# Graph attention of a two-layer model: eight probability tiles instead of four, copies six units back, and a reciprocal taken over 512 columns

## The chip, the core and the metric

The kernel runs on one core of a Trainium2 chip. The metric is the device time of one execution in microseconds (us). One execution was recorded by the hardware profiler, and its trace is what is read below. PE is the matrix engine (PEld its weight loads), DVE the vector engine, ACT the scalar engine, POOL the general engine; SP issues most of the DMAs.

## The reference

The model has two layers over `x`, four batches of 512 tokens by 512 columns. Only the first of its four blocks is touched, a two-layer graph attention with 8 heads of 64 columns:

```python
def gat_layer(x, adj, W, a_self, a_neigh, b):
    feat = jnp.einsum('nf,hfo->hno', x, W)
    attn_self = jnp.einsum('hno,ho->hn', feat, a_self)
    attn_neigh = jnp.einsum('hno,ho->hn', feat, a_neigh)
    e = attn_self[:, :, None] + attn_neigh[:, None, :]
    e = jax.nn.leaky_relu(e, LRELU_ALPHA)
    e = e + MASK_VAL * (1.0 - adj)[None, :, :]
    alpha = jax.nn.softmax(e, axis=-1)
    out = jnp.einsum('hnm,hmo->hno', alpha, feat) + b[:, None, :]
    out = jnp.transpose(out, (1, 0, 2)).reshape(out.shape[1], -1)
    return jax.nn.elu(out)
...
x = x + _L0_xattn_ref(ctx_512, _layernorm(x, axis=-1), ...)   # gat_layer twice, per batch
x = x + _L0_ffn_ref(...)
x = x + _L1_xattn_ref(...)
x = x + _L1_ffn_ref(...)
```

The mask `adj` is the normalised `x` itself, so every element of the 512 x 512 scores is used. Everything is float32 in this block.

## The kernel before

`graph_attention` is the first stage of five; a barrier stands between it and the mixture of experts that follows. Its work is cut into 256 **units**: 8 phases (4 batches times 2 layers; the order is layer 0 of batches 0 and 1, layer 1 of the same, then the same for batches 2 and 3), in each phase 8 heads, in each head 4 tiles of 128 tokens. Eight units, that is two heads, make a **pair**; there are 32 pairs, 4 in a phase.

All engines run the same hand-written loop over n, the unit, and each engine's queue is in program order. One unit goes through: `add_neighbours` on POOL (L283, a ring of LAG = 4 tiles `near`); `relu` on ACT (L459, two PSUM banks, issued two units ahead and behind the exponential of unit n in ACT's queue); `masked` on DVE (L544, makes `eneg` and its minimum); the exponential on ACT (L474, into `prob`, a ring of 4, with the row sums into `rsum`); four transposes on PE (L365, two PSUM banks `pt_bank`, each waiting until DVE has copied the unit two before); `copy_probT` on DVE (L553), which DVE issues COPY_LAG = 3 units after that unit's `masked`.

Once per pair, `finish` does the rest, spread over steps counted from the end of the pair's last unit. DVE takes the reciprocal of the pair's 128 x 8 row sums (L561, step 1). PE turns it into a 128 x 512 tile by eight 128 x 64 matmuls against the identity, with a broadcast operand (L383, step 2; float32 matmuls leave two records each, so x16), and ACT copies that to `rall` (L486). PE multiplies probabilities and features into `o_bank` (L397, steps 4 and 5, sixteen records). DVE multiplies `o_bank` by `rall` (L566, step 8), makes `zmax` (L570, step 9), ACT takes an exponential in place (L491), DVE joins them (L577, step 11). In layer 1 PE turns the result back (L405, step 13), DVE adds the old tokens (L582, step 15), and POOL stores them by DMA (L270) and loads the next ones (L265).

Beside this, `prepare(k, n)` makes the next phase's inputs during the current phase: on PE a product with the attention vectors (L338 for a layer 1, n from 10), four small transposes (L345, n = 17), the features (L355, one product a unit from n = 15 to 30 when the next phase is layer 1, four in all when it is layer 0); on DVE L534 (n = 16) and L537 (n = 18); on ACT the copies of the features (L442, n = 19, 23, 27, 31), each of which waits for the PE product of the unit before. In phases 0, 3 and 4 DVE, ACT and POOL also normalise the mask of a later batch (L511 to L527, L446, L261), and in phase 0 DVE weighs the second layer's weights (L503, L505).

Of the kernel before, what the change touches and what calls it, by code (L numbers as in the profile page):

```python
# [11 lines left out]
P = 128  # L12
RING = 2
# [5 lines left out]
ACT = mybir.ActivationFunctionType  # L19
# [56 lines left out]
def graph_attention(nc, x, ctx_dram, W0, a_self0, a_neigh0, b0, W1, a_self1, a_neigh1, b1, t_dram, x1):  # L76
# [13 lines left out]
    COPY_LAG = 3  # L90
    PREP_FIRST, PREP_FEAT = 10, 15
# [7 lines left out]
    def out_pair(pr):  # L99
        half, rest = divmod(pr, 2 * SLOTS * PAIRS)  # L100
        return half * SLOTS * PAIRS + rest - SLOTS * PAIRS

# [3 lines left out]
    with ExitStack() as stack:  # L106
# [102 lines left out]
        with nc.Block() as block:  # L209
# [39 lines left out]
            def _(pool):  # L249
# [37 lines left out]
                for n in range(ALL_UNITS + 3 * PAIR):  # L287
# [9 lines left out]
                    pr, step = divmod(n - 3 * PAIR, PAIR)  # L297
                    if 0 <= pr < ALL_PAIRS and phase(pr // PAIRS)[1] == 1:
                        j = out_pair(pr)
                        if step == 5:  # L300
                            store_new(j)
                        if step == 7 and j + RING < OUT_PAIRS:
                            pool.wait_ge(xo_stored[j % RING], 16 * (j // RING + 1))
                            load_old(j + RING)
# [5 lines left out]
            def _(pe):  # L310
                pe.wait_ge(consts, 1)

                def prepare(k, n):
# [27 lines left out]
                    if n == PREP_FEAT + 2:  # L341
# [18 lines left out]
                def transposes(n):  # L360
                    if n >= PT_BANKS:
                        pe.wait_ge(pt_ready, n - PT_BANKS + 1)
                    pe.wait_ge(p_ready, n + 1)
                    for c in range(NT):
                        last = nc.tensor.transpose(pt_bank[n % PT_BANKS][:, c, :], prob[:, n % LAG, c * P:(c + 1) * P], ident[:, :])  # L365
                    last.then_inc(pt_ps, 1)

                def finish(pr, step):

                    k, pair = divmod(pr, PAIRS)  # L370
                    if step == 2:

                        pe.wait_ge(rinv_ready, pr + 1)
                        if pr:
                            pe.wait_ge(rall_ready, pr)
                            before = pr - 1
                            if phase(before // PAIRS)[1] == 1 and out_pair(before) >= 1:
                                pe.wait_ge(xo_ready, out_pair(before))
                            elif phase(before // PAIRS)[1] == 0 and before >= 2 * SLOTS * PAIRS:
                                pe.wait_ge(xo_ready, before // (2 * SLOTS * PAIRS) * SLOTS * PAIRS)  # L380
# [6 lines left out]
                    if step == 4:  # L387
# [5 lines left out]
                    if step in (4, 5):  # L393
                        for c in range(step % 4 * 2, step % 4 * 2 + 2):
# [6 lines left out]
                    if step == PAIR + 5 and phase(k)[1] == 1:  # L401
# [6 lines left out]
                for n in range(PREP_FIRST, UNITS):  # L408
                    prepare(0, n)
                for n in range(ALL_UNITS):  # L410
                    transposes(n)
                    if n >= PAIR:
                        finish(n // PAIR - 1, n % PAIR)
                    if n >= 2 * PAIR:
                        finish(n // PAIR - 2, n % PAIR + PAIR)
                    if n // UNITS + 1 < PHASES:
                        prepare(n // UNITS + 1, n % UNITS)
                for step in range(PAIR):
                    finish(ALL_PAIRS - 1, step)
                    finish(ALL_PAIRS - 2, step + PAIR)  # L420
                for step in range(PAIR, 2 * PAIR):
                    finish(ALL_PAIRS - 1, step)

            @block.scalar
            def _(act):
# [8 lines left out]
                def prepare(k, n):  # L434
                    batch, layer, slot = phase(k)
                    if n == PREP_FIRST + 2 and layer == 0:
# [25 lines left out]
                for n in range(PREP_FIRST, PREP_FEAT + NT + 1):  # L462
                    prepare(0, n)
                root(0)
                for n in range(PREP_FEAT + NT + 1, UNITS):
                    prepare(0, n)
                for n in range(H_BANKS):
                    relu(n)
                for n in range(ALL_UNITS + 2 * PAIR):
                    if n < ALL_UNITS:  # L470
                        act.wait_ge(e_ready, n + 1)
                        if n >= LAG:
                            act.wait_ge(pt_ps, n - LAG + 1)
                        nc.scalar.activation(prob[:, n % LAG, :], eneg[:, n % LAG, :], ACT.Exp, scale=-1.0, bias=emin[:, n % LAG:n % LAG + 1],  # L474
# [6 lines left out]
                    if PAIR <= n < ALL_UNITS + PAIR and n % PAIR == 4:  # L481
# [5 lines left out]
                    if n >= 2 * PAIR and n % PAIR == 2:  # L487
# [4 lines left out]
                    if n // UNITS + 1 < PHASES:  # L492
                        prepare(n // UNITS + 1, n % UNITS)

            @block.vector
            def _(dve):
# [32 lines left out]
                def prepare(k, n):  # L529
                    if n == PREP_FEAT + 1:  # L530
# [4 lines left out]
                    if n == PREP_FEAT + 3:  # L535
# [19 lines left out]
                def finish(pr, step):  # L555
# [11 lines left out]
                    if step == PAIR + 1:  # L567
# [3 lines left out]
                    if step == PAIR + 3:  # L571
# [6 lines left out]
                    if step == PAIR + 7 and layer:  # L578
# [9 lines left out]
                prepare(0, PREP_FEAT + 1)  # L588
                mask_statistics(0)
                prepare(0, PREP_FEAT + 3)  # L590
# [7 lines left out]
                for n in range(ALL_UNITS + 2 * PAIR):  # L598
# [4 lines left out]
                    if n >= 2 * PAIR:  # L603
                        finish(n // PAIR - 2, n % PAIR + PAIR)
                    if n >= PAIR and n < ALL_UNITS + PAIR:
                        finish(n // PAIR - 1, n % PAIR)
                    if n // UNITS + 1 < PHASES:
                        prepare(n // UNITS + 1, n % UNITS)
# [1429 lines left out]
```

## Time and profile before

| what | us |
|---|---|
| median of three runs | 2299.05 (2295.28 to 2305.4) |
| the profiled execution, its own time | 2292.93 |
| its span, first to last instruction | 2291.1 |
| graph attention, first `masked` to the end of the last L582 (29.2 to 617.9) | 588.7 |
| DVE busy in that stage | about 431 |
| PE busy in that stage | about 460 |

How to read the profile: a row of the timeline gives start, duration, engine, line and operation, and in brackets how long the engine had been idle before and what ended the idleness.
### The profile page before, as it was taken

How to read it: one execution, taken by the hardware profiler on the slowest of the kernel's cores; microseconds unless marked ns; L12 is line 12 of the kernel's file. 1: busy time of each engine (PE TensorE's matmuls, PEld its weight loads, DVE VectorE, ACT ScalarE, POOL GpSimd, SP SyncE). 2: the span in 40 equal slices, each digit the busy share in tenths (PEclk: the TensorE clock that was granted, in tenths of full speed). 3: DMA queues.
4: the chain of work that ended last, by engine and by line, in shares of the span. 5: the costliest groups of instructions: out<-in, count | busy, mean ns of one | idle time of the engine just before them, and what ended most of it. 6: DMA issues, size and time to landing. Idle time of an engine off the chain costs nothing. (4 is left out here: it accounts for less than half of the span.)

```text
span 2291.1 us, 33610 instructions
## 1 busy us (share of the span) xinstructions
PE 1850.8 (81%) x8271; PEld 911.1 (40%) x8272; DVE 1461.1 (64%) x3126; ACT 1050.8 (46%) x1893; POOL 881.7 (38%) x949
## 2 busy tenths in 40 slices
PE   5598776888547999999992388888889439999994
PEld 2343433444344555555551122222222414444442
DVE  5777766777585565555654477777775675555552
ACT  5577766777432232232323256666667422222221
POOL 5465665656402545555542211111111013444441
PEclk8799877999777999999995589999999759999997
DMA  5111211110263789888656921111111626888984
GB/s 139 51 38 38 71 59 56 38 38 29 67 211 95 178 182 232 217 190 211 113 93 170 173 54 52 52 51 51 50 50 33 230 80 178 230 226 230 230 214 107
DMA packets 202160, 275.34 MB, mean 120 GB/s; under 512 B 83500, under 2 KB 121868, under 8 KB 200972
## 3 DMA queue, kind: packets, MB, share of 16 engines
q1 hardware_dynamic: 156395, 170.72, 24.2%
q0 software_dynamic: 38544, 97.02, 21.0%
q10 hardware_dynamic: 7121, 6.44, 1.4%
q8 instruction: 43, 0.70, 0.1%
q14 instruction: 57, 0.47, 0.1%
HBM read 204.44 MB, written 73.37 MB: 121 GB/s over the span
## 5 line engine op out<-in xcount | busy, mean ns | idle before, releaser
L1891 DVE TENSOR_REDUCE a_negmax<-a_m 128x1 f32<-128x512 f32 x512 | 328.1, 686 | 108.8 <-PE a_m L1748 107.2
L283 POOL TENSOR_TENSOR g_near<-g_mask,g_tb 128x512 f32<-128x512 f32 x256 | 322.8, 1277 | 156.2 <-DVE g_emin L544 154.2
L1840 ACT ACTIVATE a_prob<-a_s 128x1024 f32<-128x1024 f32 x256 | 260.6, 1021 | 142.4 <-PE a_s L1759 134.9
L365 PE MATMUL g_pt<-g_ident,g_p 128*128 128x128 f32 x1024 | 189.6, 319 | 125.9 <-DVE g_pT L553 115.7
L1283 PE MATMUL f_gu_bank<-f_wgu,f_xT 128*128 x768 | 267.9, 492 | 6.5 <-issue 3.8
L1748 PE MATMUL a_m<-a_kT,a_qT 112*128 (+1 forms) x512 | 198.7, 399 | 72.0 <-DVE a_negmax L1891 38.7
L474 ACT ACTIVATE g_p<-g_e,g_emin 128x512 f32<-128x512 f32 x256 | 183.3, 716 | 125.3 <-DVE g_emin L544 123.4
L1249 POOL DMA_INDIRECT tokens<-f_y,f_ids x96 | 151.2, 1575 | 222.5 <-DMA tokens<-f_y,f_ids 186.1
L1283 PE MATMUL s_gu_bank<-s_wgu,s_xT 128*128 128x512 f32 x512 | 232.3, 597 | 2.3 <-ACT s_xT L1335 1.6
L365 PEld LDWEIGHTS g_pt<-g_ident,g_p 128*128 128x128 f32 x1024 | 130.7, 160 | 252.9 <-DVE g_pT L553 199.7
L544 DVE CUSTOM_DVE_ANT_0 g_e<-g_near,g_h 128x512 f32<-128x512 f32 x256 | 173.2, 677 | 58.6 <-issue 28.0
L1283 PEld LDWEIGHTS f_gu_bank<-f_wgu,f_xT 128*128 128x128 f32 x768 | 143.5, 191 | 137.3 <-issue 58.3
L553 DVE COPY g_pT<-g_pt 128x512 f32<-128x512 f32 x256 | 175.4, 685 | 14.7 <-PE g_pt L365 14.1
L1302 PE MATMUL f_y_bank<-f_wd,f_actT 96*128 x384 | 183.3, 600 | 1.5 <-DVE f_actT L1368 0.9
L1249 POOL DMA_INDIRECT tokens<-s_y,s_ids x64 | 101.6, 1588 | 198.7 <-ACT s_y L1341 198.4
L459 ACT ACTIVATE g_h<-g_tb,g_s 128x512 f32<-128x512 f32 x256 | 172.8, 675 | 0.0
L1759 PE MATMUL a_s<-a_qT,a_kT 115*128 115x512 bf16 x512 | 153.8, 383 | 1.5 <-DMA a_qT<-a_mrows 1.4
L1368 DVE COPY f_actT<-f_at_bank 96x256 f32<-96x256 f32 x96 | 40.4, 421 | 175.0 <-PE f_at_bank L1292 175.0
L1283 PEld LDWEIGHTS s_gu_bank<-s_wgu,s_xT 128*128 128x128 f32 x512 | 97.8, 192 | 125.3 <-issue 125.0
L1748 PEld LDWEIGHTS a_m<-a_kT,a_qT 112*128 112x128 bf16 x512 | 49.6, 97 | 243.4 <-DVE a_negmax L1891 162.1
L1225 POOL DMA_INDIRECT f_row<-f_x_rows,f_ids x96 | 101.9, 1062 | 106.7 <-issue 104.2
L1771 PE MATMUL a_o<-a_prob,a_val 128*32 128x512 f32 x1024 | 136.4, 605 | 0.4 <-ACT a_prob L1840 0.4
(295 smaller groups left out, 2811.5 us busy)
## 6 DMA issues: line engine op xcount, KB each, us to landing
s_wgu<-in_L_ffn_w_gate_up SPq DMA_DIRECT2D x32, 1024.0 KB, 7.5
f_wgu<-in_L_ffn_gate_up_proj SPq DMA_DIRECT2D x32, 768.0 KB, 6.0
s_wd<-in_L_ffn_w_down SPq DMA_DIRECT2D x32, 512.0 KB, 4.1
a_qT<-q_parts SPq DMA_DIRECT2D x217, 64.0 KB, 2.2
g_tb<-neighbours SPq DMA_DIRECT2D x8, 1536.0 KB, 7.6
f_wd<-in_L_ffn_down_proj SPq DMA_DIRECT2D x32, 384.0 KB, 5.4
q_parts<-p_part SPq DMA_DIRECT2D x48, 128.0 KB, 2.3
g_tb<-neighbours SPq DMA_DIRECT2D x8, 512.0 KB, 4.3
```

Of the source, the lines that this page charges most:

```text
L283: pool.tensor_tensor(near[:, n % LAG, :], mask[slot][:, local % NT, :], t_all[k % SLOTS][:, local // NT, :], ALU.add).then_inc(near_ready, 1)
L365: last = nc.tensor.transpose(pt_bank[n % PT_BANKS][:, c, :], prob[:, n % LAG, c * P:(c + 1) * P], ident[:, :])
L459: nc.scalar.activation(h_bank[n % H_BANKS][:, :], t_all[k % SLOTS][:, h, :], ACT.Relu, scale=4.0, bias=s_high[k % SLOTS][:, t, h:h + 1]).t ...
L474: nc.scalar.activation(prob[:, n % LAG, :], eneg[:, n % LAG, :], ACT.Exp, scale=-1.0, bias=emin[:, n % LAG:n % LAG + 1], accum_out=rsum[:, ...
L544: V.tensor_tensor_reduce(out=eneg[:, n % LAG, :], in0=near[:, n % LAG, :], in1=h_bank[n % H_BANKS][:, :], scale=-1.0, scalar=3.0e38, op0=A ...
L553: V.tensor_copy(probT[:, n // PAIR % RING, hh, :, t * P:(t + 1) * P], pt_bank[n % PT_BANKS][:, :, :]).then_inc(pt_ready, 1)
L1249: pool.indirect_dma_start(out=tokens, out_offset=bass.IndirectOffsetOnAxis(ap=ids[:, j:j + 1], axis=0), in_=y[j % YR][:, :], in_offset=Non ...
L1283: last = nc.tensor.matmul(gu_bank[k % TR][:, 0:F], xT[k % TR][:, c, :], wgu[:, bass.ds(place, 1), c, :].rearrange("p a f -> p (a f)"), sta ...
L1302: last = nc.tensor.matmul(y_bank[k % TR][:, :], actT[k % TR][:, c, :], wd[:, bass.ds(place, 1), c, :].rearrange("p a f -> p (a f)"), start ...
L1748: nc.tensor.matmul(m_bank[n % RING][:, :], qT[k][0:PAIR_ROWS, head, st * P:(st + 1) * P], group_keys(G, PAIR_ROWS, slice(0, N)), start=Tru ...
L1840: nc.scalar.activation(prob[n % QR][:, :, :], s_bank[n % RING][:, :, :], ACT.Exp).then_inc(p_ready, 1)
L1891: V.tensor_reduce(negmax[k % RING][:, st, head:head + 1], m_bank[n % RING][:, :], X_AXIS, ALU.max, negate=True).then_inc(m_read, 1)
```

## The change

The ring `prob` grows from 4 tiles to 8 and DVE copies a unit's transposed probabilities six units back instead of three. `rinv` becomes 128 x (4, 2, 64): DVE's reciprocal reads each of the eight sums 64 times and writes 512 columns, and PE turns it by four 128 x 128 transposes in place of the eight 128 x 64 products. The steps of `finish` move: on PE the turning of the reciprocal from step 2 to 0, the products from 4 and 5 to 2, 3 and 4 (halves, then quarters), the layer-1 transposes from 13 to 11; on ACT the copy to `rall` from 4 to 5 and the exponential of `o_bank` from 2 to 3 of the pair after; on DVE L566 from 8 to 10, L570 from 9 to 11, L577 from 11 to 13, L582 from 15 to 17. In `prepare`, PE starts at n = 8 instead of 10 and makes the small transposes at 15 instead of 17; ACT copies features at 24, 28, 32 and 36 (the last two in the next phase) instead of 19 to 31; DVE's two scalings stand at 17 and 21. POOL stores at the last unit of the pair and loads two units later, each later by two. The diff without the loops that only follow:

```diff
-    COPY_LAG = 3
-    PREP_FIRST, PREP_FEAT = 10, 15
+    PROBS, COPY_LAG = 8, 6
+    STEPS = 3 * PAIR
+    SUMS = {2: range(0, 2), 3: range(2, 3), 4: range(3, 4)}
+    PREP_FIRST, PREP_FEAT, PREP_END = 8, 15, 40
...
-        prob = sb("g_p", [P, LAG, N])
+        prob = sb("g_p", [P, PROBS, N])
...
-        rinv = sb("g_ri", [P, RING, PAIR])
+        rinv = sb("g_ri", [P, RING, NT, 2, F_OUT])
...
-                    if step == 2:
+                    if step == 0:
...
-                        for u in range(PAIR):
-                            t, hh = divmod(u, 2)
-                            last = nc.tensor.matmul(r_bank[hh * F_OUT:(hh + 1) * F_OUT, t, :],
-                                                    bass.AP(rinv, pr % RING * PAIR + hh * NT + t, [[RING * PAIR, P], [0, F_OUT]]), ident[:, :],
-                                                    start=True, stop=True)
+                        for t in range(NT):
+                            last = nc.tensor.transpose(r_bank[:, t, :], rinv[:, pr % RING, t, :, :].rearrange("p h o -> p (h o)"), ident[:, :])
...
-                    if step in (4, 5):
-                        for c in range(step % 4 * 2, step % 4 * 2 + 2):
+                    if step in SUMS:
+                        for c in SUMS[step]:
...
-                    if step == PAIR + 5 and phase(k)[1] == 1:
+                    if step == PAIR + 3 and phase(k)[1] == 1:
...
-                    t, rest = divmod(n - PREP_FEAT - NT, NT)
+                    t, rest = divmod(n - PREP_FEAT - 9, NT)
...
-                        if n >= LAG:
-                            act.wait_ge(pt_ps, n - LAG + 1)
+                        if n >= PROBS:
+                            act.wait_ge(pt_ps, n - PROBS + 1)
...
-                    if PAIR <= n < ALL_UNITS + PAIR and n % PAIR == 4:
+                    if PAIR <= n < ALL_UNITS + PAIR and n % PAIR == 5:
...
-                        V.reciprocal(rinv[:, pr % RING, :], rsum[:, pr % RING, :]).then_inc(rinv_ready, 1)
-                    if step == PAIR:
+                        V.reciprocal(rinv[:, pr % RING, :, :, :], bass.AP(rsum, pr % RING * PAIR, [[RING * PAIR, P], [1, NT], [NT, 2], [0, F_OUT]])).then_inc(rinv_ready, 1)
+                    if step == PAIR + 2:
...
-                    if step == PAIR + 1:
+                    if step == PAIR + 3:
...
-                    if step == PAIR + 3:
+                    if step == PAIR + 5:
...
-                    if step == PAIR + 7 and layer:
+                    if step == 2 * PAIR + 1 and layer:
```

## Rows read from the trace of the kernel before

**Rows 1.** Windows: length, busy us of PE, PEld, DVE, ACT, POOL, granted clock: the stage.
```profile
29.20:620.00 590.80, 459.79 (x2342) 238.76 (x2342) 431.23 (x984) 403.55 (x871) 351.46 (x299) 0.86 0.15 48
```

**Rows 2.** Waits of DVE, 30 to 620 us: total us, times, longest.
```profile
DVE g_xo L582 <- PE g_r L405: 46.0, 16, 4.4
DVE g_e L544 <- issue: 28.0, 12, 2.9
DVE g_e L544 <- ACT g_h L459: 26.1, 37, 1.7
DVE g_o L566 <- PE g_o L397: 15.8, 14, 1.3
DVE g_pT L553 <- PE g_pt L365: 14.1, 15, 2.1
DVE g_s L537 <- PE g_f L345: 9.5, 7, 1.7
DVE g_xT L577 <- ACT g_o L491: 7.2, 13, 1.2
DVE g_res L577 <- issue: 5.2, 12, 1.2
```

**Rows 3.** Groups by line, shapes apart: the reciprocals of DVE, three widths.
```profile
L1381 DVE RECIPROCAL f_den<-f_den 128x192 f32<-128x192 f32 x96 | 129.9, 1353 | 3.3
L1381 DVE RECIPROCAL s_den<-s_den 128x256 f32<-128x256 f32 x64 | 112.2, 1753 | 2.2
...
L561 DVE RECIPROCAL g_ri<-g_rs 128x8 f32<-128x8 f32 x32 | 6.0, 189 | 0.0
```

**Rows 4.** Windows by pair, from one reciprocal of L561 to the next.
```profile
162.68:179.73 17.05, 16.38 (x80) 7.43 (x79) 12.36 (x30) 12.72 (x29) 10.17 (x8) 1.00 0.00 0
...
211.39:230.30 18.91, 17.54 (x91) 8.39 (x90) 12.68 (x31) 12.03 (x27) 10.14 (x9) 1.00 0.30 111
...
406.72:420.31 13.59, 9.65 (x66) 5.19 (x64) 11.94 (x30) 11.84 (x27) 10.10 (x9) 1.00 0.00 0
...
557.63:574.04 16.41, 12.49 (x70) 7.47 (x68) 12.54 (x31) 11.98 (x27) 11.50 (x11) 0.80 0.12 34
```

**Rows 5.** Timeline of DVE inside one pair with features being prepared.
```profile
169.28 0.68 DVE L544 CUSTOM_DVE_ANT_0 g_e<-g_near,g_h 128x512 f32<-128x512 f32 x1
...
169.88 0.69 DVE L553 COPY g_pT<-g_pt 128x512 f32<-128x512 f32 x1
...
177.05 0.70 DVE L566 TENSOR_TENSOR g_o<-g_o,g_rall 128x512 f32<-128x512 f32 x1 [1.09 <-PE g_o L397]
177.66 0.68 DVE L544 CUSTOM_DVE_ANT_0 g_e<-g_near,g_h 128x512 f32<-128x512 f32 x1
```

**Rows 6.** Timeline of ACT: a feature copy waiting for PE.
```profile
162.28 0.60 ACT L442 ACTIVATE g_feat<-g_f 128x512 f32<-128x512 f32 x1 [3.37 <-PE g_f L355]
```

**Rows 7.** Timeline of PE, at full clock and then at half.
```profile
174.99 1.94 PE L397 MATMUL g_o<-g_pT,g_feat 128*64 128x512 f32 x8
...
184.49 1.09 PE L383 MATMUL g_r<-g_ident,g_ri 128*64 128x128 f32 x16
...
575.45 2.32 PE L365 MATMUL g_pt<-g_ident,g_p 128*128 128x128 f32 x8 [1.28 <-DVE g_pT L553]
577.70 1.98 PE L383 MATMUL g_r<-g_ident,g_ri 128*64 128x128 f32 x16
```

**Rows 8.** Windows of 1.7 us, PE alone: busy, granted clock.
```profile
571.60:573.30 1.70, 0.66 (x4) 1.00 0.00 0
...
575.00:576.70 1.70, 1.16 (x5) 0.50 0.51 154
...
580.10:581.80 1.70, 1.70 (x9) 0.62 0.00 0
```

**Rows 9.** Timeline of DVE: its last two additions of the stage.
```profile
612.37 0.69 DVE L582 TENSOR_TENSOR g_xo<-g_r,g_xo 128x512 f32<-128x512 f32 x1 [4.42 <-PE g_r L405]
...
617.20 0.69 DVE L582 TENSOR_TENSOR g_xo<-g_r,g_xo 128x512 f32<-128x512 f32 x1 [1.27 <-PE g_r L405]
```

More of the change, by code:

```diff
@@ L101, in out_pair, with pairs_at, preparing_at @@
         return half * SLOTS * PAIRS + rest - SLOTS * PAIRS
+    def pairs_at(n):
+        return [pr for pr in range(n // PAIR - 3, n // PAIR) if 0 <= pr < ALL_PAIRS]
+    def preparing_at(n):
+        return [k for k in (n // UNITS, n // UNITS + 1) if 0 < k < PHASES]
     def mask_phase(m):
@@ L286, in _ @@
                     mask_tile(0, t)
-                for n in range(ALL_UNITS + 3 * PAIR):
+                for n in range(ALL_UNITS + 5 * PAIR):
                     if n < ALL_UNITS:
@@ L296, in _ @@
                             load_old(j)
[L297 to L304, printed above, removed]
+                    for back in (3, 4):
+                        pr = n // PAIR - back
+                        if 0 <= pr < ALL_PAIRS and phase(pr // PAIRS)[1] == 1:
+                            j = out_pair(pr)
+                            if back == 3 and n % PAIR == PAIR - 1:
+                                store_new(j)
+                            if back == 4 and n % PAIR == 1 and j + RING < OUT_PAIRS:
+                                pool.wait_ge(xo_stored[j % RING], 16 * (j // RING + 1))
+                                load_old(j + RING)
                 for r in range(RING):
@@ L364, in transposes @@
                     for c in range(NT):
-                        last = nc.tensor.transpose(pt_bank[n % PT_BANKS][:, c, :], prob[:, n % LAG, c * P:(c + 1) * P], ident[:, :])
+                        last = nc.tensor.transpose(pt_bank[n % PT_BANKS][:, c, :], prob[:, n % PROBS, c * P:(c + 1) * P], ident[:, :])
                     last.then_inc(pt_ps, 1)
@@ L375, in finish @@
                             pe.wait_ge(rall_ready, pr)
[L376 to L380, printed above, removed]
-                        for u in range(PAIR):
-                            t, hh = divmod(u, 2)
-                            last = nc.tensor.matmul(r_bank[hh * F_OUT:(hh + 1) * F_OUT, t, :],
-                                                    bass.AP(rinv, pr % RING * PAIR + hh * NT + t, [[RING * PAIR, P], [0, F_OUT]]), ident[:, :],
-                                                    start=True, stop=True)
+                            turned = sum(1 for p in range(pr - 1) if phase(p // PAIRS)[1] == 1)
+                            if turned:
+                                pe.wait_ge(xo_ready, turned)
+                        for t in range(NT):
+                            last = nc.tensor.transpose(r_bank[:, t, :], rinv[:, pr % RING, t, :, :].rearrange("p h o -> p (h o)"), ident[:, :])
                         last.then_inc(r_ps, 1)
-                    if step == 4:
+                    if step == 2:
                         pe.wait_ge(pt_ready, PAIR * (pr + 1))
@@ L406, in finish @@
                         last.then_inc(ot_ps, 1)
-                for n in range(PREP_FIRST, UNITS):
+                for n in range(PREP_FIRST, PREP_END):
                     prepare(0, n)
[L410 to L422, printed above, removed]
+                for n in range(ALL_UNITS + STEPS):
+                    if n < ALL_UNITS:
+                        transposes(n)
+                    for pr in pairs_at(n):
+                        finish(pr, n - PAIR * (pr + 1))
+                    for k in preparing_at(n):
+                        prepare(k, n - UNITS * (k - 1))
             @block.scalar
@@ L529, in prepare @@
                 def prepare(k, n):
-                    if n == PREP_FEAT + 1:
+                    if n == PREP_FEAT + 2:
                         dve.wait_ge(stT_ps, k + 1)
@@ L597, in _ @@
                 dve.wait_ge(bias_done, 1)
-                for n in range(ALL_UNITS + 2 * PAIR):
+                for n in range(ALL_UNITS + STEPS):
                     if n < ALL_UNITS:
@@ L602, in _ @@
                         copy_probT(n - COPY_LAG)
[L603 to L608, printed above, removed]
+                    for pr in pairs_at(n):
+                        finish(pr, n - PAIR * (pr + 1))
+                    for k in preparing_at(n):
+                        prepare(k, n - UNITS * (k - 1))
                     w = n - (UNITS - 2 * FC)
```

22 lines of the change are left out of this document (11 added, 11 removed).

## The prediction

> **What bounds the kernel now.** The first view is the windows by stage: the change touches only the graph attention, 591 us of the 2291 us span, and in it no engine is full, PE 460 us busy, DVE 431, ACT 404, POOL 351 [rows 1]. So the stage is bound by hand-overs between queues, and the next view is who waits for whom. DVE is the engine to follow: all others wait for it in nearly every unit, and each pair's work ends in it. Its waits [rows 2] add up to about 155 us with the small ones: 46.0 for the layer-1 transposes (L582), 28.0 in front of `masked` with no engine named, 26.1 in front of `masked` for ACT's relu, 15.8 for the products (L566), 14.1 for transposes of probabilities, 9.5 for the small transposes, 12.4 in front of L577 (7.2 + 5.2).
>
> The windows by pair give the same as a budget [rows 4]. A pair takes 13.6 us where nothing is prepared in layer 0, 16.4 in layer 1, 17.05 and 18.9 where features are prepared; DVE is busy for 11.9 to 12.7 us of each. The rest, 1.7 to 6.2 us, is what a better order can give back. PE is busy for 16.4 to 17.5 us in the pairs with features, 9.7 in the light ones.
>
> **The reciprocal, the largest term.** L561 takes 189 ns for 8 columns. Two wider reciprocals of this trace take 1353 ns for 192 and 1753 ns for 256 columns [rows 3]: 400 ns for 64 columns, 6.25 ns a column. For 512 that is 1753 + 256 x 6.25 = 3353 ns; started from the 8-column row it is 189 + 504 x 6.25 = 3339. The input with repeated elements reads no more than the wider ones did, and I see no row that would make it cheaper or dearer; I take 3.35 us. DVE gains 3.16 us a pair, 32 x 3.16 = **+101 us**. As a bound I let it go 5% either way (96 to 106).
>
> This trace shows 6.25 ns a column. The Trainium skill, page "VectorE: DVE Perf Modes", section "First, the fixed hardware budget", says that the reciprocal is an iterative division with a repeat count of 8, and gives DVE's clock as 0.96 GHz; read as eight cycles a column, that would be an estimate of 512 x 8 / 0.96 = 4.27 us, and the sum would be some 29 us worse. The trace does not agree with that reading.
>
> Nothing hides this work. It stands in DVE's queue, at unit 1 of each pair; behind it wait `masked` of the next unit (and so ACT's exponential and relu, POOL's ring) and the next copy (and so PE's transposes). DVE's budget for a pair becomes 11.9 + 3.2 = 15.1 us in layer 0 and 12.5 + 3.2 = 15.7 us in layer 1, against 13.6 to 18.9 now.
>
> **What PE saves** is real but off the path. The sixteen records of L383 took 1.09 us at full clock [rows 7]; four transposes start about 0.55 us apart, group after group. That is 0.5 us a pair, 17 us in all, on an engine that mostly waits for DVE. I count it at 0; where features are prepared it is part of what lets the pair shrink.
>
> **What the moved steps give back.** I walk the queues with the steps of the trace: `masked` 0.60 and copy 0.61 from start to start, 0.61 for L566 [rows 5].
> - L582 waited 2.9 us each time, since PE issued its transposes at step 13, after a transpose group that DVE had only just released, and DVE wanted them at 15. Now they are at 11 and 17, so they end about when the copy that DVE does before L582 can start. 46.0 less the drain's waits (4.42 + 1.27 in [rows 9], and an estimated 3.7 for the one before them, between these two and the mean of 2.9) is 36.6: all gone, **-37**.
> - L566 waited for the products at steps 4 and 5, issued two to four units earlier on DVE's clock. Now the last quarter is at 4 and L566 at 10, while the copies are three units later: one unit of margin is gained. **-16**.
> - L537 comes six units after its transposes instead of one, of which three go to the later copies: **-9.5**. L577 comes two units after ACT's exponential as before, but that exponential is no longer behind a late zmax or a feature copy: **-12**.
> - The relu: ACT idled up to 3.37 us for a feature product [rows 6], with the relu behind it. The copies of the features go from one unit behind the product to six, three of them used up by PE's later place. I take 18 of 26.1: **-18**. The rest I leave, as ACT's own pace: its exponential, its read of the sums and its relu together take more than DVE's 1.21 us a unit.
> - The 28 us with no name are the rows where POOL turns the mask tile by tile between DVE and its own additions in phases 0, 3 and 4. Order and count are the same: **0**.
> - The ring of eight removes ACT's wait for the transposes four back. No wait of that kind stood ahead of DVE's, so it is worth 0 alone; it is what allows copies six back.
> Sum of what is given back: 37 + 16 + 9.5 + 12 + 18 = **-92 us**.
>
> **What is added as waits.** While DVE divides, copy n-5 is late. From the end of copy n-6 to that of n-5 it is 3.34 + 0.60 + 0.61 = 4.5 us, in which PE may do at most two groups of transposes (two banks) and what stands with them.
> - In the pairs with features PE has a backlog: it is busy for 16.4 us now, tails of its groups included [rows 4], so about 15.9 against DVE's 15.1. But three PE units (products 1.9, 1.0, 1.0, from the 1.94 of a half in [rows 7]) fall together where DVE runs its fastest units. By the walk DVE waits 0.6 us there, just in front of the reciprocal; eight such pairs, +5.
> - In the light pairs PE has nothing to do for 4 us and then one group of 0.66 us per 1.2 to 1.9 us until the products. Today a stretch of that kind drops the granted clock: PE was busy for 0.66 us in 1.7 [rows 8] for about 5 us, the clock fell from 1.00 to 0.50, and only some 5 us of full work brought it back; meanwhile eight transposes took 2.32 us and the sixteen records of L383 1.98 instead of 1.09 [rows 7]. The thin stretch is now some 6.5 us, in nearly every light pair, layer 0 too, where it was 3.4 us and the clock stayed at 1.00 [rows 4]. At half clock a half of the products takes 3.5 us instead of 1.9, and DVE's copy of the third unit waits. The walk gives 0.5 to 2.7 us; I take 1.3 for ten pairs, +13, and 2 for the four pairs where PE also has the L338 products in the same units, +8.
>
> The Trainium skill, page "TensorE: Matmul & The Clock Gate", section "HAM oscillation — how this bites in real kernels", describes a kernel whose matrix engine dropped to half clock in every round because of a regular idle gap. It speaks against this change: where it holds, the +21 of the last item stands, and where it does not, that term is 0.
>
> Together +26, in place of the 14.1 us of waits for transposes that stand at the same spots now: **+12 us** (bounds: -14 if PE never is late, +54 if each of 27 pairs pays 2.5 us, the walk's upper end, less the 14).
>
> **The drain.** The stage ends with a serial chain [rows 9]. Three more copies are behind the last `masked` (1.8 us), and the last reciprocal, already counted, is in the chain. **+2**; bounds 0 and +6. The start issues three copies less before the first pair and is counted there.
>
> **Sum**: 101 - 92 + 12 + 2 = **+23 us**, 1.0% of the kernel. Against the profiled execution's own time it is 2292.9 + 23 = 2316; the median of the three runs is 6.1 us above that execution, and what is compared is medians, so 2299 + 23 = **2322 us**.
>
> **Rivals.**
> 1. *Not slower: the waits go and the clock holds.* If PE never falls to half clock, the added waits are 5 instead of 26, and the 14.1 us go with them: 101 - 92 - 9 + 2 = +2, 2301 us. For it: pairs of layer 0 kept 1.00 with PE busy for 9.65 of 13.59 us [rows 4]. Against: the thin stretch doubles. It decides at whether PE's clock is at 1.00 when the first products of a light pair start. Chance 0.22.
> 2. *Faster: DVE becomes full.* All waits but the drain's and the mask's go, 155 - 9 - 28 = 118 us: 101 - 118 + 2 = -15, and the relu's pace, hidden in "busy" at about 0.1 us in some units, could add as much again: 2270 to 2284 us. It needs every hand-over right in 31 pairs and a full clock, or a reciprocal that is cheaper than its neighbours. Chance 0.12.
> 3. *PE at half clock bounds the pairs.* With 2.5 us of waiting in all 27 pairs: 101 - 92 + 54 + 2 = +65, 2364 us. Against: with features prepared PE is full and keeps 1.00 [rows 4]. Chance 0.06.
> 4. *The division is eight cycles a column*, as the page named above can be read. As a mechanism of this kernel, from rows: each reciprocal would be longer by a fraction of the 3.35 us, and if by a quarter, 32 x 0.84 = 27 us on DVE's path, 2349 us. [Rows 3] speaks against it. Chance 0.04.
>
> **How the numbers follow.** The forecast case has 0.56 and its own range of 2306 to 2345. The measurement tells about 0.5%, 11.5 us, from no change. Of the forecast's 0.56, 0.06 lies under +11.5; with rival 1 that is 0.28 for the same; rival 2 is 0.12 faster; 0.50 + 0.06 + 0.04 = 0.60 slower. The range is **2286 to 2354**: it takes in rivals 1 and 4 and leaves out most of rivals 2 and 3.
>
> **What would show it.** Right: L561 at 3.35 us and DVE busy in the stage at some 530 us; no waits of L582 for L405 but in the drain; ACT's 50 us of waiting for features mostly gone; light pairs of layer 0 longer than 13.6 us, at 15 to 17; pairs with features shorter, near 16 to 17; PE's clock below 1.00 in light pairs, with DVE's copies waiting for L365. Wrong: an L561 clearly off 3.35 us; waits for transposes beyond 40 us; or pairs at DVE's bare 15.1 us.

## The result and the profile after

| | before | after |
|---|---|---|
| median us | 2299.05 (9 runs, 2295.28 to 2305.4) | 2308.52 (9 runs, 2303.83 to 2313.36) |
| the profiled execution, its own time | 2292.93 | 2313.36 |
| its span | 2291.1 | 2311.6 |
| graph attention, first `masked` to the end of the last addition | 588.7 | 601.7 |

The ratio is 1.0043, with a 95% interval of 1.0033 to 1.0052: the changed kernel is slower by 9.5 us (8 to 12). The forecast was 2322, +23 us: the sign was right, the size more than double what was measured.

The two profiled executions differ by more than the medians, 20.4 us: 13.0 of them in the stage, 1.6 before it (the first `masked` starts at 30.8 us instead of 29.2), and the rest in the four later stages. What comes behind the graph attention took between 1672.5 and 1684.0 us in the thirteen profiles of this case, in no order that follows the changes, so a difference of some us between two profiled times says nothing by itself.

Line numbers have moved: `masked` is L542, the copy L551, the reciprocal L559, its turning on PE L389, the transposes L374, the products L401, the addition of the old tokens L580. First the groups by line of the changed kernel, in the first 720 us: count, busy us, mean ns of one, idle us before it and who ended it.

```profile
L551 DVE COPY g_pT<-g_pt 128x512 f32<-128x512 f32 x256 | 175.5, 686 | 35.2 <-PE g_pt L374 35.1
...
L559 DVE RECIPROCAL g_ri<-g_rs 128x512 f32<-128x512 f32 x32 | 107.0, 3343 | 0.0
...
L389 PE MATMUL g_r<-g_ident,g_ri 128*128 128x128 f32 x128 | 27.9, 360 | 0.0
```

The wide reciprocal takes 3343 ns, between the two estimates drawn from [rows 3] (3339 and 3353); it adds 107.0 - 6.0 = 101.0 us to DVE. Next the waits of DVE in the changed kernel's stage, which answer to [rows 2].

```profile
DVE g_pT L551 <- PE g_pt L374: 35.1, 32, 2.7
DVE g_e L542 <- issue: 26.4, 12, 2.9
DVE g_e L542 <- ACT g_h L457: 7.1, 19, 1.0
...
DVE g_xo L580 <- PE g_r L409: 5.1, 2, 4.3
DVE g_e L542 <- POOL g_near L291: 3.5, 4, 2.0
DVE g_o L564 <- PE g_o L401: 1.3, 1, 1.3
```

Against [rows 2], the addition waits 5.1 us instead of 46.0 (the two that are left are the drain's), the products 1.3 instead of 15.8, the relu 7.1 instead of 26.1, the scaling behind the small transposes (L537 before, L535 now) nothing instead of 9.5. ACT's waits for the feature products went from 49.9 us to 14.6. Waits for the transposes of probabilities grew from 14.1 to 35.1. Last, windows of single pairs in the changed kernel: length, busy us of PE, PEld, DVE, ACT and POOL, granted clock.

```profile
150.51:170.21 19.70, 16.93 (x68) 8.40 (x66) 15.73 (x32) 11.64 (x25) 10.15 (x8) 0.83 0.31 109
...
410.03:426.17 16.14, 12.50 (x56) 6.67 (x54) 14.99 (x30) 13.47 (x31) 10.77 (x9) 0.79 0.00 0
...
170.21:186.12 15.91, 15.56 (x70) 7.35 (x68) 14.98 (x29) 12.40 (x29) 10.02 (x8) 1.00 0.00 1
```

DVE is now busy for 15.0 us of a 15.9 or 16.1 us pair. In the light pairs it has become the fullest engine; in the pair with features PE, busy for 15.56 of 15.91 us, is fuller still. The light pair of layer 0 that took 13.59 us in [rows 4] takes 16.14; the pair with features that took 17.05 takes 15.91. The second pair of a phase with features, 19.70 us, is the worst in this profile; PE's clock is 0.83 of full there.

**The ledger.** In the stage, DVE busy plus DVE waits is the length. Before: 431.2 + 157.4 = 588.6. After: 523.0 + 79.6 = 602.6, within 1 us of the stage's 601.7. (Both waits are summed over all rows of the view, the small ones too.) So busy grew by 92 and the waits shrank by 78.

### The profile page after: what moved, and what is told of

Read it like the earlier page. It is cut to its first block and busy times, and to the rows that moved or that the text cites. A ratio compares the mean times of both kernels' runs of the same rounds, so it can differ in the third digit from the quotient of the medians.

```text
span 2311.6 us, 32838 instructions
## 1 busy us (share of the span) xinstructions
PE 1848.7 (80%) x7887; PEld 900.5 (39%) x7888; DVE 1553.9 (67%) x3126; ACT 1049.2 (45%) x1893; POOL 882.2 (38%) x949
## 5 line engine op out<-in xcount | busy, mean ns | idle before, releaser
L374 PE MATMUL g_pt<-g_ident,g_p 128*128 128x128 f32 x1024 | 195.3, 323 | 145.0 <-DVE g_pT L551 140.1
L374 PEld LDWEIGHTS g_pt<-g_ident,g_p 128*128 128x128 f32 x1024 | 135.3, 163 | 288.8 <-DVE g_pT L551 225.1
L551 DVE COPY g_pT<-g_pt 128x512 f32<-128x512 f32 x256 | 175.5, 686 | 35.2 <-PE g_pt L374 35.1
L542 DVE CUSTOM_DVE_ANT_0 g_e<-g_near,g_h 128x512 f32<-128x512 f32 x256 | 172.7, 675 | 37.9 <-issue 26.4
L1755 PE MATMUL a_s<-a_qT,a_kT 115*128 115x512 bf16 x512 | 154.0, 383 | 3.6 <-DMA a_qT<-a_mrows 3.5
L401 PE MATMUL g_o<-g_pT,g_feat 128*64 128x512 f32 x512 | 144.5, 668 | 1.4 <-DVE g_res L575 1.4
```

Source lines behind the costliest of these rows:

```text
L542: V.tensor_tensor_reduce(out=eneg[:, n % LAG, :], in0=near[:, n % LAG, :], in1=h_bank[n % H_BANKS][:, :], scale=-1.0, scalar=3.0e38, op0=A ...
L551: V.tensor_copy(probT[:, n // PAIR % RING, hh, :, t * P:(t + 1) * P], pt_bank[n % PT_BANKS][:, :, :]).then_inc(pt_ready, 1)
```

## The experiments

All times are medians, beside runs of the kernel before on the same chip (2297 to 2299 us).

### The two halves of the change, each alone

```diff
 narrow_recip: the changed kernel with
...
-                        for t in range(NT):
-                            last = nc.tensor.transpose(r_bank[:, t, :], rinv[...], ident[:, :])
+                        for u in range(PAIR):
+                            last = nc.tensor.matmul(r_bank[...], bass.AP(rinv, ..., [[RING * PAIR, P], [0, F_OUT]]), ident[:, :], ...)
...
-                        V.reciprocal(rinv[:, pr % RING, :, :, :], bass.AP(rsum, ..., [[RING * PAIR, P], [1, NT], [NT, 2], [0, F_OUT]]))
+                        V.reciprocal(rinv[:, pr % RING, :], rsum[:, pr % RING, :])
...
 wide_old_order: the kernel before, with the reverse of these edits and nothing else
```

> The changed kernel with the reciprocal and its turning undone: L559 takes 8 columns again (0.19 us for 3.34) and PE turns it by eight broadcast products; ring of eight, copies six back and all steps stay. Theory A (the order gives back some 95 us of DVE's waits, and the wide reciprocal sits in DVE's full queue and costs nearly its whole 101 us): 2308.5 - 101 and about 20 us of waits come back where PE's own work, 16 to 17 us a pair with features, now ends last: some 2225 us, 3.6% below the changed kernel and 3.2% below the one before. Theory B (the order gives little by itself, and the reciprocal is hidden behind PE): within 1% of the changed kernel, 2285 to 2310.

> The kernel before with only the wide reciprocal and the four transposes, in the old order. Theory A: DVE gains 101 us and PE catches up during the division, which takes away the 14 us of waits for transposes and some of the 46 us in front of L582: 2299 + 75 to 95, about 2385. If the two parts add up, this one's distance from the kernel before equals that of the changed kernel from the one with the narrow reciprocal. Theory B (hidden behind PE and the waits): under 2330.

Measured: the new order with the narrow reciprocal takes **2239.33 us** (ratio to before 0.9746, 0.9732 to 0.9761), the old order with the wide one **2400.70** (1.0439, 1.042 to 1.0458). Theory B falls: the order is worth 59 us, and the wide reciprocal undoes it. Theory A has the direction of both, but misses both sizes, with 2225 expected for the first and about 2385 for the second: the two parts do not add as it had them. On the old order the wide reciprocal costs 102 us, all of DVE's added 101; on the new order it costs 2308.5 - 2239.3 = 69 us. In the old order PE does not use the division to catch up: DVE's waits stay at 163 us over all rows (157 before), the addition's 48.9 us among them.

The waits of DVE with the narrow reciprocal say why the new order is different (here L554 is the copy, L567 the multiplication of the products, L460 the relu).

```profile
DVE g_pT L554 <- PE g_pt L374: 42.6, 39, 2.1
...
DVE g_o L567 <- PE g_o L404: 8.5, 20, 1.3
DVE g_e L545 <- ACT g_h L460: 7.9, 17, 1.8
```

The order took away most of the same waits as in the changed kernel, but a part came back as waiting for PE's transposes, 42.6 us. All rows together are 99.3 us of waits, against 79.6 with the wide reciprocal; DVE is busy for 427.3 us, against 523.0. One pair with features shows the bound: length, then PE busy, the same number.

```profile
149.96:166.03 16.07, 16.07 (x82) 8.01 (x80) 12.15 (x29) 12.89 (x29) 10.14 (x8) 1.00 0.00 0
```

That pair takes 16.07 us with the narrow reciprocal and 15.91 with the wide one. So in a pair where PE is full the wide form as a whole costs nothing. That does not say that the division alone is hidden: the wide form also gives PE four transposes in place of sixteen records, and the last experiment below, with the short DVE work and PE's four transposes, does this pair in 15.29 us. In the light pairs the wide form costs most of the division's 3.2 us: the two of layer 0 that take 15.57 and 16.14 us in the changed kernel (15.19 and 15.19 in its second profile) take 12.80 and 14.00 here, and the first two without any preparation in the last phase 12.91 and 13.86 instead of 16.75 and 16.91 (15.83 and 16.39).

### Twice the division

```diff
...
+                        V.reciprocal(rinv[...], bass.AP(rsum, ...)).then_inc(rfirst_done, 1)
+                        dve.wait_ge(rfirst_done, pr + 1)
                         V.reciprocal(rinv[...], bass.AP(rsum, ...)).then_inc(rinv_ready, 1)
```

> The changed kernel with the wide reciprocal done twice (second one waits for the first), nothing left out; DVE gains another 32 x 3.3 = 106 us. From 8 columns to 512 the first 101 us of DVE cost 69 us of time. Theory E (below a certain load DVE's added work replaces waiting for PE, above it DVE is full): the second dose costs nearly all of its 106 us, at least 95, 2405 to 2420, and the waits for transposes do not grow by more than 10 us. Theory F (a fixed share of any added division is hidden behind PE): it costs about 70 us again, 2380.

Measured 2415.87 us, 107 above the changed kernel (2308.5), for 108 us of added DVE work (busy in the stage 630.6 against 523.0); waits for transposes 35.9 us, as before it. That is what Theory E had: beyond the load of the changed kernel each further us of DVE costs a us. The step from the narrow form to the wide one cost 69 us for 101 us of division, the next 107 cost 107. Theory E puts the missing 32 us down to DVE's load; the saving on PE, which came with the first step and not with the second, is a rival that this run does not separate (see the narrow reciprocal with a wide copy, below).

### Is it the clock? PE kept busy

```diff
-                    for c in range(NT):
+                    light = n % UNITS < 15 or n % UNITS == UNITS - 1 or (n // UNITS) % 4 in (0, 3)
+                    for c in list(range(NT)) * ({5: 3, 6: 3, 7: 3, 0: 2}.get(n % PAIR, 1) if light else 1):
                         last = nc.tensor.transpose(pt_bank[n % PT_BANKS][:, c, :], ...)
```

> The changed kernel with PE kept busy in its thin stretches: where no feature product follows, the transposes of the pair's units 5, 6 and 7 are done three times over and those of unit 0 twice, into the same bank; 768 transposes less those in feature units are added, and nothing is left out. Theory A1 (DVE's 35 us of waits for transposes come from PE at half clock): PE's clock in the pairs of layer 0 rises from 0.8 to near 1.0 and these waits fall to about 15 us, the whole to about 2290. Theory A2 (they come from PE's amount of work where products stand together): the clock rises, the waits stay at 35 us or grow, 2305 to 2325.

Measured **2291.45 us** (12 runs; ratio to before 0.9974, 0.996 to 0.9988): 17 us less than the changed kernel, by adding 672 transposes that compute nothing new. Waits for transposes fell from 35.1 to 19.5 us. The timeline of PE in the changed kernel shows what it cures, in the pair of 19.70 us:

```profile
153.36 0.66 PE L374 MATMUL g_pt<-g_ident,g_p 128*128 128x128 f32 x4
155.64 0.66 PE L374 MATMUL g_pt<-g_ident,g_p 128*128 128x128 f32 x4 [1.62 <-DVE g_pT L551]
157.44 1.10 PE L374 MATMUL g_pt<-g_ident,g_p 128*128 128x128 f32 x4 [1.15 <-DVE g_pT L551]
...
158.99 2.08 PE L364 MATMUL g_f<-g_w,g_xT 128*128 128x512 f32 x2
```

DVE divides from 150.5 to 153.9 us, and the copies behind the division come late. PE works on until 154.0 and then has one group of 0.66 us after 1.62 us of idleness and the next after 1.15; at 157.4 us its clock is at half (a group takes 1.10 us instead of 0.66, a feature product 2.08 instead of 1.02), and the dear work of the pair starts at that clock.

The fall does not come every time. In the second profile of the changed kernel the same two gaps stand at the same place of the same pair, and the clock holds:

```profile
156.56 0.66 PE L374 MATMUL g_pt<-g_ident,g_p 128*128 128x128 f32 x4 [1.62 <-DVE g_pT L551]
158.36 0.66 PE L374 MATMUL g_pt<-g_ident,g_p 128*128 128x128 f32 x4 [1.15 <-DVE g_pT L551]
...
159.29 1.12 PE L364 MATMUL g_f<-g_w,g_xT 128*128 128x512 f32 x2
```

So a single pair proves nothing, as this one takes 19.70 us in one profile and 16.57 in the other, and the first two pairs of the four phases in which features for layer 1 are prepared have to be taken together (us from one reciprocal to the next):

| | the changed kernel | its second profile | PE kept busy |
|---|---|---|---|
| first pair of the phase | 17.88, 19.26, 17.88, 19.26 | 19.25, 18.27, 18.69, 18.85 | 16.92, 16.91, 16.91, 16.92 |
| second pair | 19.70, 17.17, 19.70, 17.17 | 16.57, 18.64, 18.14, 18.74 | 16.56, 17.16, 16.57, 17.16 |

These eight pairs take 148.0 and 147.2 us without the edit and 135.1 with it, at full clock in all eight.

```profile
149.80:166.36 16.56, 15.54 (x84) 8.15 (x82) 15.46 (x31) 11.50 (x25) 10.07 (x8) 1.00 0.36 128
```

Theory A1 stands. The rule of the Trainium skill that the prediction weighed ("TensorE: Matmul & The Clock Gate", section "HAM oscillation — how this bites in real kernels") is borne out in kind: in the first profile a group of transposes went from 0.66 to 1.10 us behind the two gaps, and the cure was worth 17 us. It does not hold in every round here, as the second profile shows.

### The same, with the narrow reciprocal

The same edit of the transposes in the version with the narrow reciprocal.

> Narrow reciprocal in the new order, with PE's transposes repeated in the thin stretches. The version with the narrow reciprocal has 42.6 us of DVE waiting for transposes. Theory C (PE's amount of work in pairs with features sets those waits, its clock little): the waits stay at 35 us or more, 2230 to 2245. Theory D (the clock sets them, as in the changed kernel): they fall by 15 us or more, to about 2222.

Measured 2241.51 us, within the spread of the version without it (2239.33), and the waits for transposes stay at 42.6 us. That is Theory C's outcome: without the long division the edit wins nothing. It does not show that no clock is lost there, for the added transposes also cost PE time: of the pairs of one phase one fell from 16.32 to 15.16 us and its neighbour rose from 15.45 to 15.78. What the two runs show is the balance, 17 us won with the wide reciprocal and none with the narrow one.

### The division in four pieces

```diff
-                    if step == 1:
-                        dve.wait_ge(p_ready, PAIR * (pr + 1))
-                        V.reciprocal(rinv[:, pr % RING, :, :, :], ...).then_inc(rinv_ready, 1)
+                    if 1 <= step <= NT:
+                        ...
+                        t = step - 1
+                        V.reciprocal(rinv[:, pr % RING, t, :, :], bass.AP(rsum, pr % RING * PAIR + t, [[RING * PAIR, P], [NT, 2], [0, F_OUT]])).then_inc(rinv_ready, 1)
...
-                        pe.wait_ge(rinv_ready, pr + 1)
+                        pe.wait_ge(rinv_ready, NT * (pr + 1))
```

> The changed kernel with the wide reciprocal in four pieces of 128 columns, at steps 1, 2, 3 and 4 instead of all at 1. A piece costs about 0.19 + 120 x 0.00625 = 0.94 us, so DVE's work grows by about 0.2 us a pair, 6 us. Theory A1 (the 3.3 us block starves PE, its clock falls, and DVE then waits 35 us for transposes): the pieces never starve it, those waits fall to about 15 and the clock in the light pairs is above 0.9: 2295 to 2300. Theory A2 (only DVE's load counts, the place does not): 2312 to 2318.

Measured 2322.25 us, 14 above the changed kernel. A1 fell: the waits for transposes grew to 46.9 us instead of falling to 15. A2 missed too, by 4 us and in its reason: DVE's busy time as a whole did not grow (523.0 us in the stage, as in the changed kernel), only its waits did. The pieces themselves took the foreseen 6 us more, 110.2 us against 104.3 from start to next start, and other steps shrank by as much. The timeline of PE in a light pair:

```profile
422.36 0.66 PE L374 MATMUL g_pt<-g_ident,g_p 128*128 128x128 f32 x4 [2.02 <-DVE g_pT L551]
423.22 1.11 PE L389 MATMUL g_r<-g_ident,g_ri 128*128 128x128 f32 x4 [0.20 <-DVE g_ri L561]
...
427.22 3.16 PE L401 MATMUL g_o<-g_pT,g_feat 128*64 128x512 f32 x8
```

The pieces do not spare PE: it gets single groups of 0.66 us with 1.9 and 2.0 us of idleness before them, instead of the 1.1 to 1.2 us in a light pair of the changed kernel, and the clock is at half all the same when the products begin (3.16 us for a half that takes 1.94 at full clock). The last piece, at step 4, also makes PE wait for it, 4.9 us in all. In both places that were tried the division thins PE's work.

### Two moved steps put back, one at a time

```diff
 turn_back_at_13
-                    if step == PAIR + 3 and phase(k)[1] == 1:
+                    if step == PAIR + 5 and phase(k)[1] == 1:
...
 features_at_7
-                    t, rest = divmod(n - PREP_FEAT - 9, NT)
+                    t, rest = divmod(n - PREP_FEAT - 7, NT)
...
```

> The changed kernel with one moved step put back: PE's transposes of the layer-1 result at step 13 again instead of 11, DVE's L580 still at 17. Theory G (the 41 us that went from L582's waits are due to these two steps of margin): the waits of L580 for L409 come back at 2 to 3 us in each of 14 pairs, 28 to 42 us; PE catches up meanwhile and DVE's waits for transposes shrink by some 10 us; 2309 + 20 to 30, about 2334. Theory H (DVE's longer pair already gives PE the time): L580 waits less than 10 us in all, 2309 to 2315.

> The changed kernel with ACT's four feature copies two units earlier (offset 7 instead of 9, at n = 22, 26, 30, 34; 6 is the least that does not lock the queues). Theory G (ACT waited for PE's products with the relu behind it, and the margin is what cured it): ACT's waits for features rise from 15 to some 45 us and DVE's waits for the relu from 7 to 20 us or more: 2320 to 2330. Theory H (the longer pair hides it): within 3 us of the changed kernel.

Measured 2356.76 us for the first (+48 on the changed kernel, more than expected) and 2325.32 for the second (+17). The waits of DVE, first kernel and then second:

```profile
DVE g_xo L580 <- PE g_r L409: 52.2, 16, 5.3
DVE g_pT L551 <- PE g_pt L374: 34.8, 32, 2.1
```

```profile
DVE g_e L542 <- ACT g_h L457: 33.7, 26, 4.1
...
DVE g_pT L551 <- PE g_pt L374: 23.1, 22, 2.6
```

Theory G stands for both steps. Two units of margin for the addition are worth 47 us of its own waits (52.2 against 5.1), more than the 28 to 42 expected, and the 10 us by which waits for transposes were to shrink did not come (34.8 against 35.1). Two units of the feature copies are worth 27 us of waits for the relu, of which 12 come back as shorter waits for transposes; ACT's own waits for the features rise from 4.0 to 26.7 us in the stage.

### A narrow reciprocal and a wide copy

```diff
...
+                        V.reciprocal(rnar[:, pr % RING, :], rsum[:, pr % RING, :]).then_inc(rnar_ready, 1)
+                        dve.wait_ge(rnar_ready, pr + 1)
+                        V.tensor_copy(rinv[:, pr % RING, :, :, :], bass.AP(rnar, ..., [[RING * PAIR, P], [1, NT], [NT, 2], [0, F_OUT]])).then_inc(rinv_ready, 1)
```

> The new order with the reciprocal over 8 columns, then a DVE copy that repeats it to 512 columns, and PE's four transposes as in the change: the same operand for PE at about 0.19 + 0.4 to 0.7 us of DVE a pair instead of 3.34. Theory C (with the narrow reciprocal PE's amount of work ends last where features are prepared): PE saves 0.5 us a pair, DVE gains 0.3 to 0.6: the version with the narrow reciprocal and eight products (2239.3) plus or minus 5 us. Theory E' (DVE's load is all): 2239 + 10 to 20.

Measured 2242.56 us (ratio to before 0.9759), against 2239.33 with eight products, as Theory C had it. Four transposes in place of the sixteen records take waits for transposes from 42.6 to 28.7 us and all waits of DVE from 99.3 to 76.5, and the added copy, with DVE busy for 453.8 us instead of 427.3, takes it back. The pair with features that took 16.07 us:

```profile
157.92:173.21 15.29, 15.29 (x70) 7.57 (x68) 12.59 (x31) 12.91 (x29) 10.14 (x8) 1.00 0.00 1
```

This run is also the fair partner of the changed kernel, for PE does the same work in both. DVE's busy time differs by 69 us (453.8 and 523.0), the waits by 3 (76.5 and 79.6), and the medians by 66 us. From here up to `twice` nearly every us of DVE costs a us. So the 32 us that were missing between the narrow form and the wide one lie between narrow_recip and this run, where 27 us more of DVE cost 3; the four transposes came in the same step, and no run here parts what they saved from what was hidden.

### Second profiles of both kernels

> The kernel before, unchanged, for a second profiled execution: what differs between two executions of one kernel, and where. If the stage (first masked to the last L582, 588.0 us from start to start in the first profile) repeats within 1 us and the rest of the span does not, the spread of the medians comes from the four other stages; if the stage itself moves by 3 us or more, one profile can't tell the miss of my sum.

> The changed kernel, unchanged, for a second profiled execution. The first had 601.0 us for the stage (first masked to last L580, start to start), 13.0 more than the one before, against 9.8 us between the medians. If the stage repeats, 13 us is the change's own effect and the rest is noise of the other stages; if it comes out some 3 us shorter, the stage varies, most likely by when PE's clock falls.

| profile | stage, first start to last start | stage DVE busy + waits |
|---|---|---|
| before, first and second | 588.0, 588.7 | 431.2 + 157.4, 431.4 + 158.1 |
| after, first and second | 601.0, 595.6 | 523.0 + 79.6, 522.7 + 74.6 |

Medians 2296.86 and 2309.18 (ratio of the latter to before 1.0049, 1.0035 to 1.0063). The kernel before repeats its stage within 1 us; the changed one's stage moved by 5 us, with DVE's busy time unchanged, waits for transposes at 32.2 instead of 35.1, and PE busy for 447.8 us instead of 453.8 with the same instructions, at a mean clock of 0.85 instead of 0.84. The changed kernel's stage is longer by 7 us in the second pair of profiles, 13 in the first, and the medians' 9.5 lies between.

## Why the prediction was right or wrong

**The length of the division: right.** 3343 ns against 3.35 us, +101.0 us on DVE.

**That nothing hides it: right for the old order, not shown for the new.** In wide_old_order the wide form cost 102 us. In the new order it cost 69 against narrow_recip, but 66 for 69 us of DVE's work against narrow_then_copy, where PE's work is the same. The first difference therefore holds PE's saving as well, which I had put at 0: in the new order the sixteen records were something that DVE waited for. My sum did not need this price, as it went by terms against the kernel before, and it is not where the miss arose.

**The waits given back: 92 foreseen, about 96 measured.** By row: 41 for the addition (foreseen 37), 14.5 for the products (16), 9.5 (9.5), 12.4 in front of the join (12), 19 for the relu (18). Two of the five were tested by putting the step back, and returned 47 and 27 us of waits.

**The added waits: right in kind, in part in the wrong place.** I had +12 over the old 14.1; measured +18 and +21 in the two profiles. I expected the fallen clock in light pairs (1.3 us each) and put 0.6 us on each pair with features, for I held PE to be full and at full clock there. Measured waits for transposes were 0 to 1.5 us in the light pairs of layer 0 and 1 (2.7 in the last but one), 2.9 to 4.3 in the four pairs with the products that are L338 before and L347 now (foreseen 2), 0.6 in the third pair of those phases, as foreseen, and up to 4.0 in the second, where the division falls on PE's thin units before the features begin. Kept busy, PE gave 17 us back.

**All waits together: right, in part by luck.** Foreseen -92 + 12 = -80; measured -78 and -84. The added waits came out 6 to 9 us above what I had, and the ones given back 4 us above, with 2 more from small rows that I left alone; the errors cancel.

**The step that failed is the first term of the sum: DVE's growth.** I took the division's +101 as DVE's whole growth and left busy time otherwise alone. It grew by 92 (431.2 to 523.0). The reciprocals did what was foreseen (start to next start, 100.5 us more over the 32), and other steps shrank by 9 us. Seven of them lie behind the copies. Two pairs of rows of the kernel before show how, a copy with a wait behind it and one without:

```profile
597.49 0.69 DVE L553 COPY g_pT<-g_pt 128x512 f32<-128x512 f32 x1 [0.16 <-PE g_pt L365]
598.36 0.69 DVE L544 CUSTOM_DVE_ANT_0 g_e<-g_near,g_h 128x512 f32<-128x512 f32 x1 [0.18 <-ACT g_h L459]
...
603.94 0.68 DVE L553 COPY g_pT<-g_pt 128x512 f32<-128x512 f32 x1
604.54 0.69 DVE L566 TENSOR_TENSOR g_o<-g_o,g_rall 128x512 f32<-128x512 f32 x1
```

The second successor starts 0.60 us after its copy started, 0.08 before the copy's end. The first waited, and starts 0.87 us after, of which the bracket lists only 0.18: the overlap is lost too and counts as busy. Over the 256 copies, idle time taken off, a successor with a listed wait starts 0.685 us after the copy and one without 0.603. Before, 93 copies had such a successor, after, 17; another 26 before and 17 after were followed by an instruction, nearly always `masked`, some 0.1 us late with nothing listed; that ACT's relu came just in time there is my reading, which no row shows. The mean went from 0.643 us to 0.616, which is 7 us. So a wait behind a copy that a better order removes gives back 0.08 us more than its row says, and I had priced the waits by their rows. The other 2 us are small differences in several lines, the largest 1.4 us at L503 (L501 now), for which I have no cause.

The old order with the wide reciprocal keeps its waits and this pace with them (91 and 16 of the copies, a mean of 0.640; 529.5 us busy, +98), and the new order with the narrow reciprocal loses a part of it (33 and 19; 427.3 us busy, 4 below the kernel before). I had seen the pace and put it into rival 2 as an extra; the mean could be had from the view that gave [rows 5].

**The drain**: +2 foreseen. The last reciprocal is in the chain and three copies stand behind the last `masked`, as said; from the last `masked` to the last addition it was 18.8 us before (598.4 to 617.2) and 23.5 after (608.3 to 631.8). That is +4.7, of which the division, counted elsewhere, is 3.2; the rest is 1.5. In the second profiles it is 18.9 and 21.6, +2.7, so that the rest is -0.5. The foreseen 2 is neither confirmed nor refuted.

**The sum again, with the measured terms**: 101 - 9 - 78 = +14, and with the second profile 101 - 10 - 84 = +7, against +23. 9 us is the lost overlap, which the sum did not have. The two profiles lie 5 us apart with the same instructions and another PE clock. The later start of the stage, 1.3 to 1.6 us, was in no term. The 9.5 us between the medians lie between the two sums; how the last few us divide between the clock and the later stages stays open.

**The rivals.** The measured 2308.5 us lies nearer to rival 1 (2301) than to the forecast, and yet rival 1 is not what happened: in the light pair of 16.14 us the clock was at 0.50 from 418 to 422 us, just before the first products. A clock that holds was made by keeping PE busy, and came out at 2291. 2 was wrong in sign, but its extra was real, some 7 us. 3 was refuted: no 27 pairs at 2.5 us. 4 was refuted by the 3343 ns, and with it the reading of the Trainium skill, page "VectorE: DVE Perf Modes", section "First, the fixed hardware budget", as eight cycles a column (an estimate of 4.27 us).

## What to carry to other kernels

When the engine whose waits are removed is also the one that gets more work, count both in one ledger, busy plus waits equal to the stage, and measure its steps from start to start: behind each wait an overlap is lost that no row of waits lists. Before accepting a dearer form of an operation for the sake of a neighbour's, run each half alone: here the order was worth 59 us and the wide reciprocal cost 69, to save PE some 14 to 21 us of busy time, a saving that a narrow reciprocal and a copy had for 3. A gap in a helper engine's work can cost more than its own length, when its clock falls behind it; repeats of work that it has in hand are a cheap test of whether that is so. And where a clock falls in one execution and not in the next, compare sums over many pairs, not one pair.

## What the runs showed of the hardware

- DVE's reciprocal took about 6.25 ns a column: 943 ns for 128, 1353 for 192, 1753 for 256, 3343 for 512. The first and the last read each element 64 times, and were no cheaper for it.
- A DVE copy of 512 float32 columns out of an input that repeats each element 64 times took 943 ns, against 686 for the copies from PE's banks: 

```profile
L563 DVE COPY g_ri<-g_rn 128x512 f32<-128x512 f32 x32 | 30.2, 943 | 1.1
```

- An instruction behind one of DVE's copies started 0.603 us after it when it did not wait, 0.08 us before the copy's end, and at the copy's end or later when it did.
- Adding transposes that compute nothing new made the kernel 17 us faster. One kernel's stage moved by 5 us between two executions although every engine's work was the same, and in one pair the clock fell behind two gaps in one execution and held behind the same two in the other; the kernel before moved by less than 1 us.
